# Decoder layer on one core: an instruction plan with searched priorities, 14 groups of context kept, initial loads in another order

## The reference, cut to what matters

```python
x = x + linear_attention(layernorm(x), Wq, bq, Wk, bk, Wv, bv, Wo, bo)   # causal, phi = elu + 1
x = x + softmax_attention(layernorm(x), ctx, Wq, Wk, Wv)                  # keys and values from ctx
h = silu(ln(x) @ w1.T * s1) * (ln(x) @ w2.T * s2)                         # 256 -> 1024
h = gelu(h @ h1.T * sh1); h = gelu(h @ h2.T * sh2)                        # 1024 -> 1024, twice
x = x + h @ w3.T * s3                                                     # 1024 -> 256
```

## Time and profile before

| | |
|---|---|
| median of 3 runs | 1086.01 us (1084.74 to 1088.19) |
| profiled execution | 1086.11 us, of it 1084.3 us span from the first to the last instruction |
| mean granted TensorE clock | 0.991 of full speed |
| TensorE busy | 1052.5 us, 97% |
| VectorE / ScalarE / GpSimd busy | 760.0 / 554.6 / 260.1 us |
| moved by DMA | 165.42 MB |

### The profile page before, as it was taken

One profiled execution on the slowest core, in us unless ns is written; L12 is line 12 of the kernel. 1 busy time (PEld: TensorE's weight loads), 2 busy tenths in 40 slices (PEclk: granted clock), 3 DMA queues, 4 the chain that ended last, 5 costly groups with the idle time before them and its releaser, 6 DMA issues.

```text
span 1084.3 us, 25055 instructions
## 1 busy us (share of the span) xinstructions
PE 1052.5 (97%) x9898; PEld 875.7 (81%) x9898; DVE 760.0 (70%) x1708; ACT 554.6 (51%) x871; POOL 260.1 (24%) x363
## 2 busy tenths in 40 slices
PE   6998899999999999999999999999999999999997
PEld 6897678787888878878878888788887888887886
DVE  5988987778777888868998767986589626423421
ACT  4344364654646455666454755465634663433431
POOL 3232351012410152011522111611027001500500
PEclk9999899999999999999999999999999999999999
DMA  4468677435633355243442325433254445555542
GB/s 132 151 207 288 212 236 240 131 106 181 195 109 132 121 190 177 79 151 116 172 148 89 118 72 187 129 117 110 100 177 123 135 136 181 187 187 171 179 156 72
DMA packets 72614, 165.42 MB, mean 153 GB/s; under 512 B 9904, under 2 KB 25392, under 8 KB 72496
## 3 DMA queue, kind: packets, MB, share of 16 engines
q1 hardware_dynamic: 69040, 152.26, 43.4%
q10 hardware_dynamic: 3456, 11.54, 3.4%
HBM read 140.66 MB, written 34.64 MB: 162 GB/s over the span
## 4 chain that ended last, share of the span: by engine, by line
PE 80%; DVE 10%; DMA 3%; issue 2%; POOL 2%; ACT 1%; SPq 1%; ACTq 0%; DVEq 0%; POOLq 0%
PE bank L1220 40%; PE bank L1105 7%; PE bank L1205 7%; PE bank L1240 5%; PE bank L1078 5%; PE bank L1047 4%; PE bank L1062 3%; PE bank L1052 2%; PE bank L1023 2%; DMA ctx_in<-in_ctxT 1%; PE bank L1155 1%; DVE mx L954 1%; DVE hidden_full L985 1%; DVE att_l L933 1%; DMA weight_ring<-weights_scratch 1%
## 5 line engine op out<-in xcount | busy, mean ns | idle before, releaser
L1220 PE MATMUL bank<-hidden_a,weight_ring 128*128 128x512 f32 x1024 | 251.9, 396 | 0.0
L1220 PE MATMUL bank<-hidden_b,weight_ring 128*128 128x512 f32 x1024 | 247.1, 394 | 0.3 <-DVE inexact_flag L1010 0.3
L1220 PEld LDWEIGHTS bank<-hidden_b,weight_ring 128*128 128x128 f32 x1024 | 188.2, 188 | 40.1 <-issue 1.2
L1220 PEld LDWEIGHTS bank<-hidden_a,weight_ring 128*128 128x128 f32 x1024 | 186.9, 188 | 39.5 <-issue 0.6
L822 ACT ACTIVATE hidden_full<-bank,columns_sb 128x512 f32<-128x512 f32 x128 | 88.2, 689 | 169.6 <-PE bank L1220 169.1
L671 POOL TENSOR_TENSOR ve<-mv,eps 128x1 f32<-128x1 f32 (+1 forms) x80 | 19.9, 249 | 491.9 <-DVE mv L837 491.9
L1205 PE MATMUL bank<-hidden_b,weight_ring 128*128 128x512 f32 x512 | 123.7, 396 | 1.3 <-DMA weight_ring<-weights_scratch 1.3
L1205 PEld LDWEIGHTS bank<-hidden_b,weight_ring 128*128 128x128 f32 x512 | 95.4, 190 | 22.5 <-DMA weight_ring<-weights_scratch 2.1
L710 POOL TENSOR_TENSOR hidden_a<-hidden_full,hidden_a 128x512 fp32r<-128x512 f32 x64 | 83.2, 1304 | 125.3 <-ACT hidden_a L817 123.8
L874 DVE STREAM_TRANSPOSE by_token<-bank 128x512 f32<-128x512 f32 x64 | 45.5, 711 | 87.7 <-PE bank L1078 87.6
L993 DVE TENSOR_TENSOR hidden_a<-hidden_full,hidden_a 128x512 fp32r<-128x512 f32 x64 | 44.0, 692 | 68.3 <-ACT hidden_a L828 68.1
(11 more groups left out here) (135 smaller groups left out, 1727.6 us busy)
## 6 DMA issues: line engine op xcount, KB each, us to landing
weight_ring<-weights_scratch SPq DMA_DIRECT2D x160, 512.0 KB, 3.7
weights_scratch<-in_h ACTq DMA_DIRECT2D x16, 512.0 KB, 5.5
xn3T_scratch<-hidden_b SPq DMA_DIRECT2D x16, 512.0 KB, 3.8
weight_bits<-in_h SPq DMA_DIRECT2D x32, 256.0 KB, 3.9
weight_ring<-weights_scratch SPq DMA_DIRECT2D x32, 256.0 KB, 2.8
x_in<-in_x SPq DMA_DIRECT2D x16, 256.0 KB, 2.8
xb<-in_x SPq DMA_DIRECT2D x16, 256.0 KB, 3.4
ctx_in<-in_ctxT SPq DMA_DIRECT2D x16, 256.0 KB, 4.4
```

The costliest lines, as they stand in the source:

```text
L1220: mm = eng.matmul(pbank(step, g, n)[:, :], ring[:, slot, kk * P:(kk + 1) * P], src[:, part, kk, :], start=(kk == 0 and part == 0), stop=(k ...
```

## The change

Six things change.

1. `KEPT` is 1 to 14 in place of 1 to 8. Kept work has the rank `AHEAD[0]` = 373.4 for every group in place of 60 + 6g.
2. `PITCH` goes from 42 to 61.5, and `LEAD` adds a number to the rank for each pair of engine and step, found by an offline search in the replay. Some `took` values and the replay's cost of a change of tile shape (`CHANGE`, before a flat 0.2) are other numbers.
3. `PATIENCE` 5.0 to 18.5; tiled steps are taken once three are ready (`MANY`) in place of two; `HOLD` 1.0 to 0.
4. The start's loads: after `wq`, `wk`, `wv` come `xwk`, `xwv`, the context of group 0, `bv`, x of group 1, `xb`, `bo`, `wo`, `xwq`, each with a semaphore of its own, and each waiting step waits for its own. The split order is `wq, wk, wv, xwk, xwv, wo, xwq`.
5. The staging places of the last two weights are exchanged.
6. `lin_turn` waits until VectorE's part of the previous `o_turn` has read `oT_whole` (`oT_done`), before only for ScalarE's part (`oT_hi`).

```diff
-    KEPT = range(1, 9)
+    KEPT = range(1, 15)
-    SPARE, PATIENCE, HOLD = 1, 5.0, 1.0
+    SPARE, PATIENCE, HOLD, MANY = 1, 18.5, 0, 3
-            tasks[engine, step, g, n] = (rank + t, took[engine])
-    PITCH = 42
+            tasks[engine, step, g, n] = (rank + t + LEAD.get((engine, step), 0), took[engine])
+    PITCH = 61.5
+    AHEAD = 373.4, 0
+    LEAD = {("gpsimd", "bias"): -14.1, ("gpsimd", "ctx"): -18.7, ("gpsimd", "gate_rest"): -4.2, ("gpsimd", "ln1_stats"): -3.1,
...
+            ("vector", "x_div"): 5.4, ("vector", "x_turn"): -8.3, ("vector", "xn3T"): 19.9}
-            u = 60 + 6 * g
+            u = AHEAD[0] + AHEAD[1] * g
-                    "lin_turn": [t("lin_sums", g, 2 * n + 1), a("o_turn", g - (n == 0), (n - 1) % GB)], "o_turn": [a(step, g, n)],
+                    "lin_turn": [t("lin_sums", g, 2 * n + 1), v("o_turn", g - (n == 0), (n - 1) % GB)], "o_turn": [a(step, g, n)],
+    CHANGE = {(0, 1): .1, (0, 2): .1, (1, 0): .33, (2, 0): .24, (2, 1): .14, (1, 2): .24}
-    AT = {("scalar", "split", n): (7, 7.7, 8.4, 15, 15, 15, 15)[n] for n in range(7)}
+    AT = {("scalar", "split", n): (6.2, 6.9, 7.6, 9.5, 10.5, 14.5, 15)[n] for n in range(7)}
-                patient = ff and all(now - e[2][2] < PATIENCE for e in tiled) and len(tiled) < 2
+                patient = ff and all(now - e[2][2] < PATIENCE for e in tiled) and len(tiled) < MANY
-                if kind != mode:
-                    took += .2
+                took += CHANGE.get((mode, kind), 0)
-                eng.dma_start(bvb[:, :], bv.partition_broadcast(P)).then_inc(weights["late"], 16)
-                eng.dma_start(bob[:, :], bo.partition_broadcast(P)).then_inc(weights["late"], 16)
-                eng.dma_start(xb[:, :, :], x[0:GB].rearrange("b s d -> s b d")).then_inc(xb_loaded, 16)
-                for dst, src in zip(whole[3:], (woT, xqT, xkT, xvT)):
-                    eng.dma_start(dst, src.rearrange("(c p) o -> p c o", p=P)).then_inc(weights["late"], 16)
+                for n, (dst, src) in enumerate(zip(whole, (wqT, wkT, wvT, xkT, xvT, woT, xqT))):
+                    if n == 5:
+                        load_ctx(0)
+                        eng.dma_start(bvb[:, :], bv.partition_broadcast(P)).then_inc(weights["bv"], 16)
+                        load_x(1)
+                        load_xb(0)
+                        eng.dma_start(bob[:, :], bo.partition_broadcast(P)).then_inc(weights["bo"], 16)
+                    eng.dma_start(dst, src.rearrange("(c p) o -> p c o", p=P)).then_inc(weights[SPLIT[n]], 16)
-                            eng.wait_ge(split_done, 7)
+                            eng.wait_ge(split_done, 4)
                         project(step, g, xwk, ctxs, ctx_hi, ctx_done, xk_psum)
```

More of the change, by code:

```diff
@@ L41, in put @@
         for engine, t in slots.items():
-            tasks[engine, step, g, n] = (rank + t, took[engine])
-    PITCH = 42
+            tasks[engine, step, g, n] = (rank + t + LEAD.get((engine, step), 0), took[engine])
+    PITCH = 61.5
+    AHEAD = 373.4, 0
+    LEAD = {("gpsimd", "bias"): -14.1, ("gpsimd", "ctx"): -18.7, ("gpsimd", "gate_rest"): -4.2, ("gpsimd", "ln1_stats"): -3.1,
+            ("gpsimd", "project"): -0.7, ("gpsimd", "res"): -27.5, ("gpsimd", "x_turn"): -18.9, ("scalar", "ctx"): -12.5,
+            ("scalar", "gate_round"): -12.9, ("scalar", "gelu"): 26.5, ("scalar", "k"): 21.5, ("scalar", "ln1T"): 21.2,
+            ("scalar", "ln2T"): 1.7, ("scalar", "o_turn"): 19.5, ("scalar", "q"): -27.5, ("scalar", "shift"): -18.6,
+            ("scalar", "split"): 22.7, ("scalar", "tanh"): -7.8, ("scalar", "x_exp"): 23.8, ("scalar", "xk"): -25.3,
+            ("scalar", "xn3T"): -46.6, ("scalar", "xq"): -7.9, ("scalar", "xv"): 10.7, ("sync", "keep_k"): 6.8,
+            ("sync", "keep_stats"): 60.5, ("sync", "keep_v"): 26.7, ("sync", "keep_x2"): -18.6, ("sync", "keep_xn"): -34.1,
+            ("sync", "load_ctx"): 44.2, ("sync", "load_k"): 29.7, ("sync", "load_stats"): -58.8, ("sync", "load_v"): -3.6,
+            ("sync", "load_x"): 6.6, ("sync", "load_xb"): 16.3, ("sync", "out"): 24.7, ("tensor", "gate"): 3.4,
+            ("tensor", "hidden"): -41.8, ("tensor", "k"): 53.9, ("tensor", "lin_scores"): -2.9, ("tensor", "lin_sums"): -13.8,
+            ("tensor", "ln1T"): 10.2, ("tensor", "ln2T"): 17.7, ("tensor", "max"): -29.3, ("tensor", "project"): -16.7,
+            ("tensor", "q"): -45, ("tensor", "shift"): 12.5, ("tensor", "v"): 6.7, ("tensor", "w3"): -4.8,
+            ("tensor", "x_scores"): 61.7, ("tensor", "x_sums"): -21.2, ("tensor", "x_turn"): 0.3, ("tensor", "xk"): 1.7,
+            ("tensor", "xn3T"): 10.2, ("tensor", "xq"): -3.8, ("tensor", "xv"): 11.9, ("vector", "gated"): 33.8,
+            ("vector", "gelu_rest"): -60.5, ("vector", "k"): 11.7, ("vector", "k_heads"): 0.4, ("vector", "lin_mask"): -14.3,
+            ("vector", "lin_turn"): -6.5, ("vector", "ln1"): 0.5, ("vector", "ln1T"): 21.9, ("vector", "ln1_stats"): 3.7,
+            ("vector", "ln2"): -19.4, ("vector", "ln2T"): -45, ("vector", "ln3"): -15.5, ("vector", "low_bits"): -32.3,
+            ("vector", "max_of"): -4, ("vector", "o_turn"): 14.3, ("vector", "out"): 0.9, ("vector", "project"): 9.9,
+            ("vector", "q"): 9.9, ("vector", "shift"): 0.3, ("vector", "split"): -19, ("vector", "v"): -2.2,
+            ("vector", "x_div"): 5.4, ("vector", "x_turn"): -8.3, ("vector", "xn3T"): 19.9}
@@ L74, in decoder_layer_program @@
         for b in range(GB):
-            steady("lin_scores", b, tensor=-0.28 + 4.6 * b, took=dict(tensor=.95))
+            steady("lin_scores", b, tensor=-0.28 + 4.6 * b, took=dict(tensor=.87))
             for n in range(4 * b, 4 * b + 4):
@@ L78, in decoder_layer_program @@
             for h in range(2):
-                steady("lin_sums", 2 * b + h, tensor=4 + 4.6 * b + h, took=dict(tensor=.46))
+                steady("lin_sums", 2 * b + h, tensor=4 + 4.6 * b + h, took=dict(tensor=.44))
             u = 7.2 + 4.71 * b
@@ L84, in decoder_layer_program @@
             steady("ln2", b, vector=u + 7, took=dict(vector=.4))
-            steady("max", b, tensor=23.39 + 2 * b, took=dict(tensor=.95))
+            steady("max", b, tensor=23.39 + 2 * b, took=dict(tensor=.87))
             for n in range(4 * b, 4 * b + 4):
@@ L109, in decoder_layer_program @@
         for p in range(2):
-            put("xn3T", 2 * f + p, 0, FF, tensor=0, scalar=0, vector=0, took=dict(tensor=.44, scalar=1.05, vector=.6))
+            put("xn3T", 2 * f + p, 0, FF, tensor=0, scalar=0, vector=0, took=dict(tensor=.4, scalar=1.05, vector=.6))
             for n in range(2):
@@ L415, in decoder_layer_program @@
             xwq, xwk, xwv = (sb(n, [P, 2, C, D], F32R) for n in ("xwq", "xwk", "xwv"))
-            split = (wq, wk, wv, wo, xwq, xwk, xwv)
+            split = (wq, wk, wv, xwk, xwv, wo, xwq)
             ctx_in = sb("ctx_in", [P, C, T])
@@ L730, in _ @@
                     elif step == "split":
[L731 removed]
+                        eng.wait_ge(weights[SPLIT[g]], 16)
                         eng.activation(split[g][:, 0, :, :], whole[g], ACT.Copy).then_inc(split_hi, 1)
```

62 lines of the change are left out of this document (31 added, 31 removed).

## The result

The changed kernel takes 1078.80 us (median of 6 runs, 1077.57 to 1081.24) against 1086.57 us (1083.79 to 1088.19): the ratio is 0.9931, interval 0.9916 to 0.9945. It is faster by 7.8 us. The forecast was 1068 us, a gain of 18 us, so 10 us of it did not come. Of its cases, the first rival (stores gate the first turn, 1078 to 1084 us, 13%) is the one that names this time.

The account below looks back on a forecast made before the run. The prediction took TensorE as the bound, busy 1052.5 of 1084.3 us. Gains of 11 (start and kept groups), 6 (tile shapes) and 1 (small waits) made 18 us: 1086.1 - 18 = 1068 us, range 1055 to 1082.

Parts of the forecast that it names:

- the first rival: Value stores through one buffer delay the first turn's gate to T = 157: 1078 to 1084 us, chance 13%.
- The balance 0.44 * (T - 20) - 3 * N: TensorE's loss from 20 us to the first gate at T, with N kept groups: 8.6 us for T = 135, N = 14.
- The ring loads took no harm: After 140 us, six more groups' reloads beside ring loads were taken to cost TensorE 0, upper bound 28 us.
- patience starve the attention: Rival: tiled steps wait longer, so later turns' gates wait; 1103 us at 5 us per turn, chance 10%.
- Fewer changes of tile shape: From 125 to 930 us, patience removes one in seven of 235 changes at 0.18 us each: 6 us gained.
- term for start and kept groups: Up to the first gate, earlier attention and kept work replacing idle time and low clock: 11 us gained, T = 135.
- the gates did not run ahead of the stores: Before the first turn, gates can run a few us ahead of `tanh`, which waits for the last `keep_v`; hence T = 135.
- term for small waits: Small waits of TensorE between 20 and 80 us: 1 us gained.
- the ranks are worth 0: From 140 to 940 us `LEAD` and `PITCH` gain 0, since only 3.6 us of idle is there; bounds of -3.
- The forecast's signs: Signs of being right, mostly before the first gate: early `xv`, kept rounds 7 to 8 us apart, fewer than 220 shape changes.

Follow-up runs that it names:

- experiment on patience: The changed kernel with `PATIENCE` 5.0 and two ready tiled steps enough, as before: 1089.09 us, ratio 1.0021.
- nudges: One replay duration changed by 10 ns, no setting changed: on the changed kernel 1088.98, 1083.49 and 1083.32 us; on the kernel before 1087.52 and 1087.29 us.
- the run with the old loads: The changed kernel with only SP's first transfers in the order of before, semaphores and all other orders kept: 1080.86 us, ratio 0.9944.
- 8 kept: The changed kernel with 8 kept groups in place of 14: 1089.73 us, ratio 1.0034.
- before, 14 kept: The kernel before with 14 kept groups and nothing else changed: 1092.47 us, ratio 1.0051.
- both parts: The kernel before with the new start's loads and 14 kept groups, ranks and patience as before: 1082.04 us, ratio 0.9943.
- the ring late: The changed kernel with the four first ring loads held from 84 to 125 us in SP's list, other engines' orders the same: 1076.19 us, ratio 0.99.
- new start alone: The kernel before with only the new start's loads, semaphores, split order, staging and `lin_turn` wait: 1091.85 us, ratio 1.0042.
- their nudge: The kernel before with new start and 14 kept groups, plus replay duration `max_of` changed from .60 to .61: 1083.81 us, ratio 0.9971.
- copies moved by 12 us: The changed kernel with the first ring loads held until 125 us and weight copies from the fourth on 12 us later on ScalarE: 1074.30 us, ratio 0.9883.

## Why the prediction was wrong

**What it had right.** TensorE was the bound, and the stretch before the first gate was where time could be had. The balance 0.44 * (T - 20) - 3 * N, with T = 144 and N = 14, gives 12.6 us; the chip lost 11.5 us of idle time and up to 3.6 us to the clock. The ring loads took no harm from six more `load_k`: TensorE waited for them for 1.0 us, against 1.3, so what the Trainium skill says of small transfers (DMA: Bandwidth & Descriptors, "Rules for kernel authors") cost TensorE nothing here. Nor did patience starve the attention: from 140 to 940 us all of TensorE's waits together are 5.5 us.

**The steps that failed.** The mechanism was right, but three terms of the sum were mis-sized. By the balance of the section on the result they brought 8.3 us, not 18: 3.8 us are missing in the tile shapes, 3.0 in start and kept groups, 2.9 in the small waits.

**"Fewer changes of tile shape", 6 us, was 2.2.** This is the largest miss. 12 of 235 changes went, not 34: 2.2 us by the forecast's own price. The experiment on patience agrees: 9 changes, 1.6 us. What the long patience did besides, 8 us between two orders, can't be told from a reshuffle, since nudges move the time as much.

**The term for start and kept groups, 11 us, was 8.** It measured 2.1 us in the first 20 us (1.8 in the run with the old loads), 1.1 us less idle time and up to 4.8 us of clock up to 140 us. The new start is the surer part: in the first 20 us TensorE is idle for 5.6 to 6.7 us in the thirteen profiled executions that have the new loads and semaphores, and for 7.4 us or more in the others. The size was off by T: 144, not 135. The rounds took 8.7 us, not 7.8, in part because the forecast took the round time from a stretch in which SP hadn't yet to wait behind the ring burst. Its first rival had the result, late stores, with a single buffer as the reason; shown is SP's list as a reason: with the ring loads later, T is 139.6 and 2.6 us come back, of which the forecast's balance gives 0.44 * 4.4 = 1.9. It isn't the whole reason: T is still not 135, and the rounds still take 8.1 us. And the gates did not run ahead of the stores: the last `keep_v` is issued at 138.5 us, the first gate starts 5.5 us later without a wait, where the plan has put it.

**The term for small waits, 1 us of gain, was 1.9 us of loss.** The sentence that from 140 to 940 us the ranks are worth 0, "with bounds of -3", missed what matters most there. The kernel before had 3.6 us of idle time in that window. It was read as a property of the kernel; it was one of its order. Of the eleven new orders other than before's two nudges (whose 4.4 and 3.5 us are like its own), ten have 9.3 to 12.6 us, the changed kernel's nudges among them, and one (8 kept) has 7.0; the five with TensorE's list of the changed kernel have 4.1 to 6.7. This is some 5 us by which the searched order is better than its neighbours. That the search earned it by luck among many orders or by a replay that is true in this stretch isn't settled: no run here compares the replay's waits with the chip's.

**How the parts sum.** New start and 14 kept groups on unsearched orders: 3 to 6 us (two orders). The changed kernel's settings on three unsearched orders: ratios 1.0021, 0.9973, 0.9966. The order that the search picked: 0.9931. So, as an estimate from these few orders, the mechanism that the forecast priced gives about half of the gain and the picked order the rest. Neither part of the mechanism shows alone: each alone saves 3 to 4 us early and has 7 to 9 us more of later waits. Together they save 10 to 11 us early and pay 6 to 9 later. One difference between "before, 14 kept" and the two kernels with both parts is again on SP: there the store of the statistics stands behind four ring loads and takes 11.2 us, here behind two of them, 5.9 and 6.7 us. No run holds the rest still, so this isn't shown to be the reason.

The forecast's signs: `xv` of group 0 came at 18.44 us, not before 17, since `xk` of group 0 and 40 filling matmuls now stand before it, from 14.85 us on; it came 1.7 us earlier than before and not 4; the kept rounds took 8.7 us and not 7 to 8; idle time from 80 to 120 us was 7.4 us, not below 4; the first gate missed the interval of 118 to 140 us, and the changes of shape, 223, the bound of 220.

## What to carry to other kernels

Where a list scheduler's order comes out of a replay, undo a part only with all orders held still, or nudge a duration that means nothing a few times first: here 10 ns in the replay moved the changed kernel's time by 4.5 to 10.2 us, as much as most settings seemed to be worth, though it left the kernel before where it was. A small amount of idle time after a tuned plan is a result of its order and not a floor that a new plan inherits. Before more work goes through a store and reload loop, look at what else stands in the issuing queue: one `load_stats` that waited for a small store behind a 2 MB burst, which nobody needed for 55 us, stretched one round of that loop to 16.3 us.

## What the runs showed of the hardware

A 2 KB store issued on SP behind four 512 KB loads on the same queue took 9.3 to 11.5 us to land in thirteen profiled executions, 11.4 us in the kernel before and 10.9 in the changed one. With only two of the four loads ahead of it, it took 5.9, 5.9 and 6.7 us (new start alone, both parts, their nudge). In the four kernels where the four loads were moved away from it, it took 4.4 to 4.8 us, and there the next such store, which now stands behind them, took 9.1 to 10.1 us. The first two stores with the ring late:

```profile
DMA to landing us min/median/max: 4.7/4.7/4.7
DMA to landing us min/median/max: 10.1/10.1/10.1
```

The weight copies on ScalarE's queue hardly matter for this store: one issued at 89.3 us stood beside the 4.7 us, and with none issued from 76.8 to 95.6 us (copies moved by 12 us) it took 4.4.

The granted clock may have given back as much as the idle time did: the idle time before 140 us fell by 3.2 us, and up to 4.8 us came from fewer stretches at 1.2 GHz.
